# Hidden keys struck out of the values, a plan from key sums, and context fetched from ScalarE's queue in 2 KB rows

## The reference

```python
valid = arange(6404) < length                    # length: 6404 minus a random 0..1601
mask = broadcast_to(valid[:, None, :], (1, 1024, 6404))

q = split_heads(layernorm(x) @ Wq.T + bq)
k = split_heads(ctx @ Wk.T + bk)
v = split_heads(ctx @ Wv.T + bv)
scores = einsum('bhqd,bhkd->bhqk', q, k) / sqrt(8)
scores = where(mask, finfo.min, scores)
x = x + merge_heads(softmax(scores) @ v) @ Wo.T + bo

logits = layernorm(x) @ gate_w.T                 # 8 experts, the two best of each row
x = x + sum over the two: prob * (gelu(x_norm @ w1[e] + b1[e]) @ w2[e] + b2[e])
```

## Time and profile before

| | us |
|---|---|
| median of 3 runs | 342.94 |
| the profiled execution, its own time | 343.54 |
| its span, first to last instruction | 341.8 |
| busy: TensorE / ScalarE / VectorE / GpSimd | 269.8 / 231.5 / 172.3 / 68.2 |
| opening up to the first score product | 65.8 |
| loop, to the last addition | 166 |
| gate and experts | 110 |

### The profile page before, as it was taken

One profiled execution on the slowest core, in us unless ns is written; L12 is line 12 of the kernel. 1 busy time (PEld: TensorE's weight loads), 2 busy tenths in 40 slices (PEclk: granted clock), 3 DMA queues, 4 the chain that ended last, 5 costly groups with the idle time before them and its releaser, 6 DMA issues.

```text
span 341.8 us, 6186 instructions
## 1 busy us (share of the span) xinstructions
PE 269.8 (79%) x1853; PEld 133.7 (39%) x1853; DVE 172.3 (50%) x424; ACT 231.5 (68%) x364; POOL 68.2 (20%) x110
## 2 busy tenths in 40 slices
PE   2695884799998989999999989896486059999950
PEld 2453463423221222222221212124385049999940
DVE  4587665142536354444535354546681316777722
ACT  4386436367799999999999999891577015555520
POOL 7771001000000000000000004002027703444440
PEclk9999675799999999999999999999679559999985
DMA  6999964010010100101010101069601170111105
GB/s 186 357 234 353 368 136 87 3 32 9 6 35 12 27 17 21 25 15 37 2 38 12 27 12 27 18 231 357 103 12 53 55 186 24 34 33 32 33 31 184
DMA packets 33891, 29.57 MB, mean 87 GB/s; under 512 B 15344, under 2 KB 29192, under 8 KB 33744
## 3 DMA queue, kind: packets, MB, share of 16 engines
q1 hardware_dynamic: 32304, 26.41, 26.9%
q0 software_dynamic: 1568, 2.93, 3.2%
HBM read 21.62 MB, written 7.45 MB: 85 GB/s over the span
## 4 chain that ended last, share of the span: by engine, by line
PE 33%; issue 26%; ACT 14%; SPq 11%; DMA 7%; DVE 6%; ACTq 1%; DVEq 1%; POOL 0%; POOLq 0%
PE bank L1217 7%; ACT w2T L964 7%; ACT arenaB L964 7%; PE bank L1344 6%; PE bank L1199 5%; DMA ctx_sb<-in_ctx_dram 4%; SPq L244 4%; PE bank L1352 4%; SPq L301 4%; PE bank L1191 3%; PE bank L1071 2%; PE bank L1123 1%; DVE arenaB L872 1%; SPq L274 1%; DMA arenaA<-ys_dram 1%
## 5 line engine op out<-in xcount | busy, mean ns | idle before, releaser
L691 DVE TENSOR_TENSOR arenaA<-bank,arenaA 128x512 f32<-128x512 f32 x80 | 55.2, 690 | 83.1 <-PE bank L1217 83.0
L964 ACT ACTIVATE arenaB<-bank 128x1024 f32<-128x1024 f32 x80 | 77.5, 1021 | 7.4 <-PE bank L1199 5.5
L964 ACT ACTIVATE w2T<-bank 128x1024 f32<-128x1024 f32 x80 | 76.8, 1028 | 4.4 <-PE bank L1199 3.2
L1199 PE MATMUL bank<-qS,keys 64*128 64x512 bf16 x324 | 62.7, 386 | 9.9 <-ACT w2T L964 5.0
L1199 PEld LDWEIGHTS bank<-qS,keys 64*128 64x128 bf16 x324 | 15.4, 92 | 95.4 <-ACT w2T L964 45.0
L994 ACT ACTIVATE mask_u<-bank,arenaB 128x128 f32<-128x128 f32 x92 | 26.3, 369 | 38.9 <-PE bank L1344 38.0
L1217 PE MATMUL bank<-arenaB,vcur 128*32 128x512 f32 x320 | 42.6, 605 | 1.0 <-DVE vcur L684 0.3
L1217 PE MATMUL bank<-w2T,vcur 128*32 128x512 f32 x320 | 42.6, 605 | 0.0
L382 POOL COPY arenaC<-ctx_sb 128x128 f32 x11 | 3.2, 295 | 150.2 <-PE bank L1127 150.2
L445 POOL DMA_INDIRECT ys_dram<-arenaB,mask_u x23 | 22.0, 955 | 35.7 <-DVE arenaB L878 35.7
L1344 PE MATMUL bank<-arenaB 128*128 128x128 f32 x184 | 27.7, 298 | 1.4 <-DVE arenaB L864 1.0
(11 more groups left out here) (292 smaller groups left out, 322.6 us busy)
## 6 DMA issues: line engine op xcount, KB each, us to landing
mask_u<-in_L_ffn_w_dram SPq DMA_DIRECT2D x2, 2048.0 KB, 10.5
mask_u<-in_mask_BxSxS_bk_dram SPq DMA_DIRECT2D x6, 560.5 KB, 11.3
qS<-qparts_dram SPq DMA_DIRECT2D x4, 448.0 KB
ctx_sb<-in_ctx_dram SPq DMA_DIRECT2D x2, 768.0 KB, 11.9
mask_u<-in_mask_BxSxS_bk_dram SPq DMA_DIRECT2D x6, 240.0 KB, 6.3
keys_in<-kparts_dram SPq DMA_DIRECT2D x40, 32.0 KB
mask_u<-in_mask_BxSxS_bk_dram SPq DMA_DIRECT2D x1, 1121.0 KB, 10.1
xs_dram<-w1T SPq DMA_DIRECT2D x2, 520.0 KB, 17.1
```

The source lines that it names most:

```text
L691: nc.vector.tensor_tensor(a, bank[:, 4 + k % 2, :], a, ALU.add).then_inc(s["ac"], 1)
L964: nc.scalar.activation(probs[u % 8], bank[:, 2 * (u % 2):2 * (u % 2) + 2, :].rearrange("p a b -> p (a b)"), ACT.Exp, scale=SCALE).then_inc ...
L1199: last = mm(bank[:, 2 * (u % 2) + a, :], keys[rows, g, :], qS[rows, g, cols], start=not hides, stop=True, tile_position=(64 * a, 0))
```

## The change

Context goes to ScalarE's queue, issued ahead of everything else there, with four neighbouring keys in a partition (rows of 2 KB, the last three tiles 1.5 KB); the first four tiles come from GpSimd in 97 rows of 2 KB. ScalarE's eviction restores the order of keys with a strided read of the bank. SyncE's queue has only x, the weights and the mask. The folds are replaced: the packed mask bytes are cast to bf16 (`numbers`) and TensorE sums them per key (`key_sums`), so that each key is known as hidden for all, for none or mixed (`flags`). Counts per tile come from the flags by three products. Only tiles with a mixed key are `partial`. A key hidden for all gets the factor 0 in its values and in the column of ones (`keep`). The gate's products move ahead of chunk 1, `pick` to GpSimd, the query norms and `bv_all` into the turns, the score bound and `general` behind the plan (`gen_ready`), and TensorE's placing of tile 0's keys ahead of the jump over `general`.

```diff
-CTX_CUTS = [(1, 12), (12, 24), (24, 36), (36, T)]
+CTX_CUTS = [(4, 12), (12, 24), (24, 36), (36, T)]
+ALL = 255.0 * P
...
-            context(0)
-            context(1)
-            mask_rows(0, 0, 4)
-            context(2)
-            mask_rows(0, 4, 7)
-            context(3)
+            mask_rows(0, 0, 7)
...
-            pool.wait_ge(s["ctxpad"], 1)
-            pool.dma_start(ctx_sb[PAD:P, 0, :], ctx_in[0, 0:P - PAD, :]).then_inc(s["ctx_in"], 16)
+            pool.dma_start(ctx_sb[PAD // 4:P, 0:4, :].rearrange("p j d -> p (j d)"),
+                           ctx_in[0, 0:4 * P - PAD, :].rearrange("(p j) d -> p (j d)", j=4)).then_inc(s["ctx_in"], 16)
...
+            pool.wait_ge(s["rowkey"], len(COMBOS) + 4)
+            nc.gpsimd.tensor_scalar(pick, rowkey, iota_p[:, :], None, ALU.is_equal).then_inc(s["pick"], 1)
...
+                if values:
+                    pool.wait_ge(s["vn"], before)
+                    nc.gpsimd.tensor_copy(keep[:, :], flags[:, 0, bass.ds(tile, 1)]).then_inc(s["kp"], 1)
+                    pool.wait_ge(s["kp"], 2 * before + 1)
+                    nc.gpsimd.tensor_tensor(bvk[:, :], bv_all[:, :], keep[:, :].broadcast_to([P, D]), ALU.mult).then_inc(s["kp"], 1)
...
+            def numbers(b):
...
+                nc.vector.tensor_copy(bits[b], and_acc[:, :].bitcast(U8)[:, c0 * P:c1 * P]).then_inc(s["acb"], 1)
+
+            def key_flags(b):
+
+                c0, c1 = MASK_CUTS[b]
+                sums = bank[:, 3, c0:c1]
+                dve.wait_ge(s["ks_ps"], b + 1)
+                nc.vector.tensor_scalar(flags[:, 0, c0:c1], sums, ALL - 0.5, None, ALU.is_lt).then_inc(s["pl_sb"], 1)
+                nc.vector.tensor_scalar(flags[:, 2, c0:c1], sums, 0.5, None, ALU.is_gt).then_inc(s["pl_sb"], 1)
+                dve.wait_ge(s["pl_sb"], 3 * b + 1)
+                nc.vector.scalar_tensor_tensor(flags[:, 1, c0:c1], sums, 0.5, flags[:, 0, c0:c1], ALU.is_gt, ALU.mult).then_inc(s["pl_sb"], 1)
 
...
+                nc.vector.tensor_copy(vnext[:, :, HD:HD + 1], keep[:, :].rearrange("p (h a) -> p h a", h=1).broadcast_to([P, H, 1]))
+                nc.vector.scalar_tensor_tensor(vnext[:, :, 0:HD], b6[:, 2 * P:3 * P].rearrange("p (h d) -> p h d", d=HD), keep[:, :],
+                                               bvk[:, :].rearrange("p (h d) -> p h d", d=HD), ALU.mult, ALU.add).then_inc(s["vn"], 1)
...
+            def context(k):
+                t0, t1 = CTX_CUTS[k]
+                whole = t1 - t1 % 4
+                act.dma_start(ctx_sb[:, t0:whole, :].rearrange("p (c j) d -> p c (j d)", j=4),
+                             ctx_in[0, t0 * P - PAD:whole * P - PAD, :].rearrange("(c p j) d -> p c (j d)", p=P, j=4)).then_inc(ctx_in_s[k], 16)
+                if whole < t1:
+                    act.dma_start(ctx_sb[:, whole:t1, :].rearrange("p j d -> p (j d)"),
+                                 ctx_in[0, whole * P - PAD:S2, :].rearrange("(p j) d -> p (j d)", j=t1 - whole)).then_inc(ctx_in_s[k], 16)
+
+            for k in range(len(CTX_CUTS)):
+                context(k)
...
-                    nc.scalar.activation(ctxT[:, 512 * c:512 * c + w], bank[:, c % 2, 0:w], ACT.Copy, accum_out=csums[:, c:c + 1]).then_inc(s["cc_sb"], 1)
+                    nc.scalar.activation(ctxT[:, 512 * c:512 * c + w].rearrange("p (k j) -> p k j", k=P), bank[:, c % 2, 0:w].rearrange("p (j k) -> p k j", k=P),
+                                         ACT.Copy, accum_out=csums[:, c:c + 1]).then_inc(s["cc_sb"], 1)
...
+            def key_sums(b):
+                pe.wait_ge(s["acb"], b + 1)
+                pe.wait_ge(s["const"], 12)
+                pe.wait_ge(s["qsqr"], 2)
+                c0, c1 = MASK_CUTS[b]
+                for t in range(c0, c1):
+                    last = mm(bank[:, 3, t:t + 1], bits[b][:, (t - c0) * P:(t - c0 + 1) * P], onesb[:, 0:1], start=True, stop=True)
+                last.then_inc(s["ks_ps"], 1)
+
+            def plan_counts():
+                pe.wait_ge(s["pl_sb"], 6)
+                for a in range(3):
+                    last = mm(pb[0:T, a:a + 1], flags[:, a, :], onesb[:, 0:1], start=True, stop=True)
+                last.then_inc(s["pl_ps"], 1)
...
+                if c == 10:
+                    key_sums(0)
+                if c == 12:
+                    key_sums(1)
+                if c == 13:
+                    plan_counts()
+                if c == 14:
+                    plan_places()
...
+            def first_keys(g0, g1):
+                for gg in range(g0, g1):
+                    for part in range(3):
+                        at = (part * G + gg) * P
+                        last = mm(bank[:, 4 + gg // 4, gg % 4 * P:(gg % 4 + 1) * P], pick[:, at:at + P], kparts[:, part, :], start=(part == 0), stop=(part == 2))
+                last.then_inc(s["k0_ps"], 1)
+
+            pe.wait_ge(s["kch"], 4)
+            pe.wait_ge(s["pick"], 1)
             pe.sem_inc(s["mt"], 1)
-            pe.wait_ge(s["plan_ready"], 1)
+            first_keys(0, 4)
+            mask_turn(0)
+            pe.wait_ge(s["bd"], 9)
+            mm(bank[:, 3, 64:65], ones[0:1, 0:P], bound[0:1, 3:4], start=True, stop=True).then_inc(s["bd_row"], 1)
+            first_keys(4, G)
+            pe.wait_ge(s["gen_ready"], 1)
```

269 lines of the change are left out of this document (123 added, 146 removed).

## The result

The changed kernel takes 338.8 us (median of 16 runs, 337.2 to 340.3) against 342.9 us before (16 runs): ratio 0.990, 95% interval 0.987 to 0.992. It is faster by 1.0%, clear of the noise, and not by the forecast 3.5% (331 us): inside the range of 324 to 340, outside the forecast's own, 326 to 336. The profiled execution took 337.9 us, its span is 336.2 us, against 343.5 and 341.8.

What follows compares the result with a forecast made beforehand. Prediction: ScalarE's exponentials pace the loop, TensorE's masking products tile 0, and context turns and waits shape the opening. Terms -7.2 + 1.5 - 0.9 - 5.7 = -12.3 take 342.9 to 331 us; range 324 to 340, its own 326 to 336.

Steps and rivals of the forecast that it cites:

- Tile 0 without masking products: Loop: with no partial tile, tile 0 runs like tile 1, 15.72 us instead of 22.75; -7.2 us in all.
- The jump over the first loop: Loop: TensorE must now jump over the masking-product body; +1.5 us, bounds 0 and 3.1, partly covered by exponentials.
- GpSimd's addition past the keys' copy: Loop: GpSimd's 2.37 us addition comes later and no longer stands beside a keys' copy; -0.9 us.
- Weights and norm: Opening: weights share engines with context and come 2.2 us later, sliding the layer norm's turn; +1.9 us (0.5 to 4).
- The turns: Opening: context turns at 1.43 us without waits, gate products +2.0, key sums +2.2, strided eviction free; end at 44.9 us.
- hidden with 1.2 us to spare: Opening: VectorE's work allows the second key sums at 39.5 us, before TensorE wants them at 40.7; no cost.
- Plan 46.1: Opening: the plan's list needs only 1.2 us behind the turns, so it stands at 46.1 us, against 54.3 before.
- Plan to first scores: Opening's end: 14 us from plan to first scores, at 60.1 us; 11.4 us before; opening -5.7 us overall.
- Rival 1: Opening gains nothing, only the tile does: slow eviction, late VectorE or mask, or later weights; 336.3 to 340 us, chance 0.2.
- Rival 2: Opening: GpSimd's 97 context rows fall to one DMA engine and land at 35 us, delaying everything; 350 us, chance 0.1.
- Rival 3: Opening gains more: TensorE holds 2.4 GHz behind the plan and the jumps are covered; 325 us, chance 0.12.
- Rival 4: Opening: the queue does not matter, mask and context finish no earlier; +2, 333 us, kept inside the forecast.

Runs made afterwards that it cites:

- e3: Changed kernel with tile 0 counted among the tiles whose scores get masking products, as before; 345.8 us, ratio 1.008.
- g3: Kernel before with the context's transfers, in their old rows of 512 bytes, issued at once from ScalarE's queue; 345.2 us, ratio 1.007.
- e1: Changed kernel with the context's transfers back in SyncE's queue at their old places among the mask's; 335.3 us, ratio 0.982.
- f3: Changed kernel with the weights' four transfers moved to the head of ScalarE's queue, ahead of the context's; 334.5 us, ratio 0.978.
- h2: Kernel before with the context in rows of 2 KB, issued at once from ScalarE's queue; 341.8 us, ratio 0.998.
- e2: Changed kernel with `pick` back on VectorE, between the third and fourth OR; 336.2 us, ratio 0.982.
- e4: Kernel before with `pick` moved from VectorE to GpSimd; 342.2 us, ratio 0.999.
- f1: Changed kernel with the context's transfers back in SyncE's queue and `pick` back on VectorE; 333.1 us, ratio 0.974.
- g4: Kernel before with the context in rows of 2 KB and the strided eviction, still in SyncE's queue; 339.0 us, ratio 0.987.
- h1: Changed kernel with context in SyncE's queue, `pick` on VectorE, TensorE's tile-count load earlier, GpSimd's mask copy and two ones transfers later; 329.9 us, ratio 0.965.
- g2: Changed kernel with weights first in ScalarE's queue, `pick` on VectorE, TensorE's tile-count load earlier and GpSimd's mask copy later; 331.4 us, ratio 0.965.

## Why the prediction was wrong

The forecast was -12.3 us; the profiled executions differ by 5.6, the medians by 4.1. The loop came as forecast. The opening failed, in two terms: the weights' delay, sized at +1.9, was 4.9 us, and VectorE's work with `pick`, put at nothing, held TensorE up by 2.76. Step by step, in its order:

- **Tile 0 without masking products, -7.2:** right. Tile 0 went from 22.75 to 16.1 us; masked again it costs 6.1 us by the ratios, 7.0 by the medians (e3).
- **The jump over the first loop, +1.5:** too much. ScalarE waited 0.81 us at 70.73, no more; its exponentials cover it. The full price of a jump, 3 us, did not appear.
- **GpSimd's addition past the keys' copy, -0.9:** right, all ten copies take 0.43 us. The whole loop is 7.6 us shorter, the three terms said 6.6.
- **Weights and norm, +1.9 (0.5 to 4): the step that failed first.** "The weights come some 2.2 us later" was 5.4, x 1.4 instead of 1, and the LayerNorm's turn slid by 4.9 us, past the upper bound. I had named the right mechanism, with the square root behind `qk_col`, and mis-sized it: I took the sharing as a matter of bytes in flight, and the last weight's 3.3 us to landing became 8.1. Longer rows in the other queue are not the main reason: beside context rows of 512 bytes, the weights' own length, the four took 5.5 to 7.5 us (g3). What in the sharing costs so much stays open; that the context ahead of them does it e1, f3 and h2 show, by 2.5 to 4 us of time.
- **The turns:** 1.43 us each (28.49, 29.93, 31.37 and 32.80 us), so the strided eviction is free (588 ns, was 587), as I took it. No chunk waited for context. The key sums took 1.04 for 36 and 0.53 us for 15, less than the +2.2. The gate products are 2 us, as costed.
- **VectorE, "hidden with 1.2 us to spare": the step that failed second.** VectorE was late by 2.76 us at the second key sums. The casts cost 2.56 and 1.15 us, as said (3.0 and 1.3). But `pick` took GpSimd 9.2 us and not 6.3, and costing it "at nothing" looked only at who waits for its output. It takes VectorE's time while it runs (4.65 us of one OR). e2 and e4 show it: 2.5 us by e2's ratio. GpSimd's two query pieces stretch the next three ORs as well (6.65 instead of 4.1 us), which the forecast had at 1.36 each; that is there without `pick` too (e2).
- **Plan 46.1:** came at 51.7; 45.75 with both causes removed (f1). So the rest of that count held, though partly by errors that cancel: the mask made VectorE wait 2.50 us.
- **Plan to first scores, 14 us** (the terms listed add up to 14.2)**:** 15.4 (51.9 to 67.25), 11.4 before. Most of its terms were met: key products, mask turn and bound 4.2 (57.28 to 61.48; 4.3 costed), loads and jump 4.36 (4.3 costed), the key parts' steps 1.5. VectorE came to the key parts 3.9 us behind the plan, not 3.1, with one instruction beside GpSimd's cast at 1.06 us. What no term had: TensorE enters the scores at 1.2 GHz (four products in 1.04 us, 0.61 in the earlier trace rows), with the loads and the jump right ahead of them (e3).
- **Rival 1** ("weights later than I say", 336 to 340) is the case that came, with VectorE late as well. I gave it 0.2 and called the mask's 6 us in hand an argument against; VectorE, not the mask, was what had nothing in hand. **Rival 2** is refuted: GpSimd's 97 rows landed in 6.4 us and chunk 0 did not wait. **Rival 3** did not come: the granted clock was 0.50 from 50 us to the first exponential. **Rival 4** had the queue cost 2 us at most, through a late mask; it costs 2.5 to 4, through the weights.

The accounts nearly close, in ratios of the time before (1% is 3.4 us): rows of 2 KB -1.3% (g4), the queue +1.1% (h2 against g4), tile 0 -1.8% (e3 against the changed kernel), `pick` +0.7% (e2 against it). Together -1.2%; -1.0% was measured. The +0.2% or so left for the key classes and the new order of the opening agrees with f1 beside g4: its plan stands 4.1 us earlier, its chain behind the plan is 4.4 us longer. These differences have intervals of about 0.4% each, so the last one is not shown to differ from zero, and tile 0's share may be too large by e3's low clock.

What stays open: why the turn over the `general` block takes 3.1 us and whether it could stand under TensorE's wait for the first key parts was not tried; nor was a kernel with the keys' products between jump and scores again.

## What to carry to other kernels

Before transfers are moved to a second queue "to start at once", list every small transfer that is under way then and who waits for it: here four weights that land 3.3 us after issue alone took up to 8.1 beside another queue's context. Count also what the issuing costs the engine that does it: four transfers took 14.5 us in rows of 512 bytes and 2.4 in rows of 2 KB. And an operation moved to an idle engine is not free when another engine is held up by it, as the OR was by `pick` (6.01 us instead of 1.36): ask what VectorE does during GpSimd's pass, and whether it has slack there.

## What the runs showed of the hardware

- **Issuing can block.** Four transfers of 0.7 to 0.96 MB in rows of 512 bytes held ScalarE's queue 14.5 us (g3); four of 0.5 to 0.8 MB in rows of 2 KB 2.4 us (h2). That is 6400 rows against 1408.
- **Two small transfers can slow all others.** Two of 128 KB, issued by GpSimd from 8 partitions into 8, took the whole traffic from about 400 to between 130 and 250 GB/s for 6 us; moved, the dip moved with them (h1). Which of their traits does it was not varied. In every kernel here the DMA engines show as busy in that spell. A sentence of the Trainium skill on back-pressure fits (DMA: Bandwidth & Descriptors, section Back-pressure in remote DMA): stalled writes hold up the same engine's other queues. It is written of transfers between cores; that it is the cause here was not tested.
- **Leading a queue does not secure an early landing.** The fourth weight took 4.8 us in one execution and 8.3 in another, with the same order in the queues (f3, g2). The Trainium skill says that an engine goes round its queues packet by packet (DMA: Bandwidth & Descriptors, section Queues, rings and completion order); the weights' 3.3 us alone in SyncE's queue and 8.1 beside the context agree.
- **The clock at the loop's entry** goes with what stands right ahead of it. With the keys' products there the granted clock was back at 2.4 GHz from 0.9 us ahead of the first score product to 0.7 behind (before, e4, g3, g4, h2); with 3.1 to 4.4 us of standing there, 1.1 to 2.6 us behind in nine executions, 7.6 in g2 and 9.8 in e3. Why those two are so late is not shown.
